# A two-layer decoder on one core: one table of steps per engine from the second half's expert tiles to the end of the third attention

## The reference

```python
x = x + _L0_attn_ref(_layernorm(x), ...)                      # gated recurrence and a gated FFN
x = x + _L0_xattn_ref(_layernorm(x), ctx_1024, ctx_1024, ...) # attention 1, over the context
x = x + _L0_ffn_ref(_layernorm(x), ...)                       # shared expert plus top 2 of 8 experts
x = x + _L1_attn_ref(_layernorm(x), ...)                      # attention 2, only the 24 strongest queries of a head
x = x + _L1_xattn_ref(ctx_1024, ctx_1024, _layernorm(x), ...) # attention 3, over the context
x = x + _L1_ffn_ref(_layernorm(x), ...)                       # top-1 experts with a capacity
```

```python
q_norm = jnp.sum(jnp.abs(q), axis=-1)
_, index = jax.lax.top_k(q_norm, u)            # u = 24
sel_attn = jax.nn.softmax(sel_scores, axis=-1)
attn_output = attn_output.at[bI, hI, index].set(jnp.einsum('bhut,bhtd->bhud', sel_attn, v))
```

## Time and profile before

| | us |
|---|---|
| median of three timed runs | 722.93 |
| lowest, highest | 719.76, 728.80 |
| the profiled execution | 720.38 |
| its span, first to last instruction | 718.7 |
| tiles of the second half | 299.4 to 342 |
| projections of the second attention | 342 to 394 |
| picks | 394 to 497 |
| third attention | 497 to 596 |
| what follows | 596 to 718.7 |

### The profile page before, as it was taken

The page is one execution under the profiler, slowest core; times in us unless marked ns, Lnnn a source line. Parts: engine busy times, 40 slices in busy tenths (PEclk is TensorE's granted clock), DMA queues, the critical chain, the costliest instruction groups (busy, mean ns, idle before and its releaser), DMA issues.

```text
span 718.7 us, 14894 instructions
## 1 busy us (share of the span) xinstructions
PE 569.8 (79%) x4679; PEld 413.6 (58%) x4679; DVE 434.5 (60%) x1157; ACT 290.9 (40%) x679; POOL 243.0 (34%) x364
## 2 busy tenths in 40 slices
PE   3689996889987979898727898876989984574992
PEld 1344444566764659897515686643666652454991
DVE  4879887666766575456373465554556624677443
ACT  2675422245555215454203466530435542302660
POOL 6745503301011666253640113224000002372652
PEclk9899999999999979999868899995999988577997
DMA  9974988653500166532301000363445300013114
GB/s 282 326 126 132 277 237 230 162 132 82 135 8 5 42 244 215 170 86 67 79 26 36 0 2 1 100 155 83 126 99 122 70 2 2 0 46 102 34 35 136
DMA packets 87494, 75.72 MB, mean 105 GB/s; under 512 B 10457, under 2 KB 80753, under 8 KB 84513
## 3 DMA queue, kind: packets, MB, share of 16 engines
q1 hardware_dynamic: 82544, 66.80, 34.5%
q0 software_dynamic: 3296, 6.79, 3.2%
q10 hardware_dynamic: 1584, 1.26, 0.6%
HBM read 41.59 MB, written 32.98 MB: 104 GB/s over the span
## 4 chain that ended last, share of the span: by engine, by line
PE 48%; DVE 20%; DMA 9%; issue 8%; POOL 6%; ACT 4%; SPq 3%; DVEq 1%; POOLq 0%; ACTq 0%
PE ps L2330 5%; PE ps L1864 5%; PE ps L2197 3%; PE ps L2162 3%; PE ps L2432 3%; PE ps L2444 3%; PE ps L2342 2%; PE ps L2181 2%; POOL xs_scr L839 2%; PE ps L2158 2%; DMA f<-k_scr 2%; SPq L433 2%; PE ps L2015 2%; PE ps L1860 2%; PE ps L2176 2%
## 5 line engine op out<-in xcount | busy, mean ns | idle before, releaser
L1445 DVE TENSOR_REDUCE negm<-ps 128x4 f32<-128x512 f32 x128 | 84.3, 688 | 57.1 <-PE ps L2162 53.9
L1026 ACT ACTIVATE wa<-ps 128x1024 f32<-128x1024 f32 x64 | 65.5, 1024 | 70.6 <-PE ps L2181 64.5
L2330 PE MATMUL ps<-nT,f 128*128 128x128 f32 x368 | 52.0, 288 | 2.6 <-DVE wb L1657 1.2
L2330 PEld LDWEIGHTS ps<-nT,f 128*128 128x128 f32 x368 | 47.9, 204 | 3.6 <-DVE wb L1657 1.6
L2197 PE MATMUL ps<-wa,f 128*32 128x128 f32 x1024 | 40.2, 284 | 4.0 <-ACT wa L1026 1.5
L1936 PE MATMUL ps<-identb 128*128 128x512 bf16 x100 | 34.2, 401 | 7.8 <-DVE negm L1445 3.9
L710 POOL DMA_INDIRECT x_scr<-y_tok,selT x32 | 31.9, 996 | 23.8 <-ACT stack L1134 10.7
L844 POOL DMA_INDIRECT y_scr<-f,stack x23 | 25.6, 1114 | 30.3 <-DVE f L1803 24.8
L2162 PE MATMUL ps<-stack 75*128 75x128 bf16 x352 | 35.6, 225 | 0.0
L2162 PEld LDWEIGHTS ps<-stack 75*128 75x128 bf16 x352 | 28.4, 101 | 12.2 <-issue 2.4
L1529 DVE COPY f<-w_gu 128x512 f32 x46 | 20.4, 442 | 22.0 <-issue 10.5
(11 more groups left out here) (399 smaller groups left out, 1464.8 us busy)
## 6 DMA issues: line engine op xcount, KB each, us to landing
k_scr<-parts SPq DMA_DIRECT2D x48, 192.0 KB, 3.0
q_scr<-parts SPq DMA_DIRECT2D x48, 192.0 KB, 2.8
stack<-k_scr SPq DMA_DIRECT2D x11, 600.0 KB, 7.2
stack<-q_scr SPq DMA_DIRECT2D x11, 600.0 KB, 5.5
w_w<-in_w SPq DMA_DIRECT2D x2, 2048.0 KB
wb<-q_scr SPq DMA_DIRECT2D x5, 600.0 KB
f<-k_scr SPq DMA_DIRECT2D x5, 600.0 KB
x_scr<-sel SPq DMA_DIRECT2D x2, 1472.0 KB, 10.2
```

Of the source, the lines that this page charges most:

```text
L1026: link.release(act.activation(wa[:, u % 2, :], BF[u % 2], ACT.Exp, scale=SCALE), hWA.filled, hWA.at(stage, n * 4 + u), hB.freed)
L1445: v.tensor_reduce(negm[:, g4 * 4:g4 * 4 + 4, j], A[u % 2].rearrange("p (h k) -> p h k", h=4), AX.X, ALU.max, negate=True).then_inc(hA.free ...
L2330: last = mm(A[x % 2][:, c * S:(c + 1) * S], gu_of[x % NGU][:, c * S:(c + 1) * S], nT[:, k % 2, q * S:(q + 1) * S], start=True, stop=True)
```

## The change

The loops from tile 23 to the end of the third attention are replaced by a third table, LATE, with one list for each of PE, ACT, DVE and POOL. All steps of the tiles (tg, td, tk on PE; ts, to, tn; tc, tp), of the projections (normx, turnx, evx, projq, projk, projv, tokq, heads, pick, turns, seld), of the picks (qp, pt, sc, tu, sv, pl; ex, ec, pu, at; pk, oq, lo, rc, ob; pf), of the output side and the next queries (outp, evo, back, res, stat2, rstd2, norm2, turn2, ev2, projq2, evq2, split2), of the gathers and their sums (ga, comb, stat, mrstd) and of the attention (A, B, M, V, X, o and their partners) stand in one order per engine.

So the first half's gathers are issued as soon as its rows are stored, its sums, statistics and normalisation stand among the second half's tiles, its projections follow the last tile, the picks of the first half run while the second half is gathered and projected, and the third attention's first scores run among the last picks. Normalisation moves from DVE to ACT (normx, with the mean's product in `from_mean`, two more small operations on POOL). The matmuls of `keep_warm` in the projections are gone. Memory is laid out anew: k1 and q1 lie in the stack, the picks' buffers over the gate and up weights, which adds waits for the last tile. In PSUM the first half's projections turn in three banks; the second half's, and the output side of blocks 0 to 2, take turns in bank Z, each waiting for the reader of the one before. `late_loads` has a new order and new waits.

```diff
-        k1 = [flat_gu[:, i * 2 * BT:(i + 1) * 2 * BT] for i in range(2)]
-        q1 = [flat_gu[:, (2 + i) * 2 * BT:(3 + i) * 2 * BT] for i in range(2)]
+        k1, q1 = ([room[:, (2 * i + k) * 2 * BT:(2 * i + k + 1) * 2 * BT] for i in range(2)] for k in range(2))
         spent = w["down"][:, :, :, :].rearrange("p e c d -> p (e c d)")
-        new_q, rest_q = [spent[:, s * BT:(s + 1) * BT] for s in range(2)], spent[:, 2 * BT:3 * BT]
-        pick32, q_bd, e_row, e_col, o_bd, put = ([room[:, (2 * k + s) * HU:(2 * k + s + 1) * HU] for s in range(2)]
+        pick32, q_bd, e_row, e_col, o_bd, put = ([flat_gu[:, (2 * k + s) * HU:(2 * k + s + 1) * HU] for s in range(2)]
                                                  for k in range(6))
-        pick16 = [room[:, 12 * HU + s * HU // 2:12 * HU + (s + 1) * HU // 2].bitcast(bf16) for s in range(4)]
+        pick16 = [spent[:, s * HU // 2:(s + 1) * HU // 2].bitcast(bf16) for s in range(4)]
...
+        def place(step):
+            kind, n = step[:-2], int(step[-1])
+            if kind in ("heads", "turns"):
+                return n
+            return (1 if n < 3 else 2) if kind in ("outp", "back", "turn2", "projq2") else n // 2
+        ORDER = {eng: FRONT[eng] + [s for s in WOVEN[eng] if not of_attention(s) and s[:2] not in ("fa", "fb")]
+                 + [s for s in LATE[eng] if s[:-2] in SIGNALS[eng]]
                  for eng in FRONT}
         PLACE = {step: (eng, i) for eng, steps in ORDER.items() for i, step in enumerate(steps)}
@@ -362,7 +366,23 @@
             assert len({PLACE[s][0] for s in steps}) == 1
             return max(PLACE[s][1] for s in steps) + 1
-        T_TURN = {s: k for k, s in enumerate(s for s in WOVEN["PE"] if s[0] in "MXo" and of_attention(s))}
+        T_TURN = {a: {s: k for k, s in enumerate(s for s in steps if s[0] in "MXo" and of_attention(s))}
+                  for a, steps in ((0, WOVEN["PE"]), (2, LATE["PE"]))}
+        three = (U, Bk[0][:, 0, :], Bk[1][:, 0, :])
+        first_turns, later_turns = ([s for s in LATE["PE"] if s[:-2] in READ_LATE and place(s) == n] for n in range(2))
+        def late_bank(step):
+            return (lambda: three[first_turns.index(step) % 3], lambda: Z, lambda: T)[place(step)]()
...
-                sp.wait_ge(qk1_ready, 1)
+                sp.wait_ge(gu_done, N0)
+                sp.wait_ge(pe_front, after("heads.1"))
                 load_k(a, 0, slot(0))
-                sp.wait_ge(qk1_ready, 3)
-                load_k(a, 2, slot(2))
                 store_pair("qp2", 0, queries, [], range(1))
                 sp.wait_ge(hP[0].freed, hP[0].free("qp2", 1))
+                sp.wait_ge(down_done, N0)
                 load_q(a, 0, slot(0))
+                sp.wait_ge(dve_front, after("comb.3"))
+                sp.wait_ge(slots_stored[1], 16 * PER)
+                load_k(a, 1, slot(1))
+                load_k(a, 2, slot(2))
                 store_pair("qp2", 0, queries, [], range(1, 2))
                 sp.wait_ge(hP[1].freed, hP[1].free("qp2", 1))
-                sp.wait_ge(attnT_done, 2 * B)
+                sp.wait_ge(scored, HB)
+                sp.wait_ge(q_picked, HB)
                 load_q(a, 1, slot(1))
-                load_k(a, 1, slot(1))
+                store_m(a, 0, slot(0))
+                sp.wait_ge(scored, B)
+                sp.wait_ge(q_picked, B)
                 load_q(a, 2, slot(2))
-                store_m(a, 0, slot(0))
+                store_m(a, 1, slot(1))
                 store_pair("qp2", 1, queries, [], range(1))
-                store_m(a, 1, slot(1))
+                load_stack(a, 3, slot(3))
+                store_m(a, 2, slot(2))
                 store_pair("qp2", 1, queries, [], range(1, 2))
-                for n in range(3, NSTEP):
+                for n in range(4, NSTEP):
...
+            def gathers(b):
+                h = b // HB
+                g.wait_ge(slots_stored[h], 16 * PER)
+                for k, dst in enumerate((y_tok, second)):
+                    g.indirect_dma_start(dst[:, b, :], None, x0_scr[h],
+                                         bass.IndirectOffsetOnAxis(ap=pos0_i[:, k * B + b:k * B + b + 1], axis=0))\
+                     .then_inc(rows_back[b // GB], 16)
+            def pick_copy(b):
+                g.wait_ge(gu_ready, N0)
+                g.wait_ge(pick16_ready, b + 1)
+                if b > 1:
+                    g.wait_ge(q_picked, b - 1)
+                g.tensor_copy(pick32[b % 2], pick16[b % 4]).then_inc(pick32_ready, 1)
...
-                    for n in range(NSTEP):
-                        for j in range(2):
-                            copies(n, j)
-                        if n == 0:
-                            late_step("h2", 3)
-                            late_step("s2", 2)
-                            late_step("s2", 3)
+                    for s in LATE["POOL"]:
+                        kind, n = s.split(".")
+                        if of_attention(s):
+                            copies(int(n), int(s[1]))
+                        elif kind == "clear":
+                            g.wait_ge(gu_done, N0)
+                            chain.settle()
+                            clear()
+                        elif kind == "ga":
+                            gathers(int(n))
+                        elif kind == "pf":
+                            pick_copy(int(n))
+                        else:
+                            late_step(kind, int(n))
...
-            for h in range(2):
-                if h == 1:
-                    for n in range(2):
-                        block_stats("qp1", n)
-                g.wait_ge(slots_stored[h], 16 * PER)
-                for b in range(h * HB, (h + 1) * HB):
-                    for k, dst in enumerate((y_tok, second)):
-                        if h == 0:
-                            g.wait_ge(slot_out, NT0 + b * TOPK + k + 1)
-                        g.indirect_dma_start(dst[:, b, :], None, x0_scr[h],
-                                             bass.IndirectOffsetOnAxis(ap=pos0_i[:, k * B + b:k * B + b + 1], axis=0))\
-                         .then_inc(rows_back[b // GB], 16)
-            for n in range(2, NBLK):
-                block_stats("qp1", n)
-            for b in range(B):
-                g.wait_ge(pick16_ready, b + 1)
-                if b > 1:
-                    g.wait_ge(q_picked, b - 1)
-                g.tensor_copy(pick32[b % 2], pick16[b % 4]).then_inc(pick32_ready, 1)
-                if b == 9:
-                    late_step("h2", 0)
-                elif b == 13:
-                    late_step("s2", 0)
-                    late_step("h2", 1)
-            late_step("s2", 1)
-            late_step("h2", 2)
...
+                if kind == "comb":
+                    v.wait_ge(rows_back[n], 16 * GB * TOPK)
+                    for k, src in enumerate((y_tok, second)):
+                        for b in range(n * GB, (n + 1) * GB):
+                            last = v.scalar_tensor_tensor(out=x_tok[:, b, :], in0=src[:, b, :], scalar=wts[:, k, b:b + 1],
+                                                          in1=x_tok[:, b, :], op0=ALU.mult, op1=ALU.add)
+                        link(last, settle=True)
+                    v.sem_inc(dve_front, 1)
...
+                this = "%s.%d" % (kind, n)
+                bank, where = late_bank(this), place(this)
+                if where == 2:
+                    settled("T")
+                    pe.wait_ge(q_bd_ready, B)
+                    pe.wait_ge(hT.freed, hT.at("ac2", T_next[0]))
+                    held["T"] = reader(this)
+                else:
+                    turns, depth = (first_turns, 3) if where == 0 else (later_turns, 1)
+                    turn_no = turns.index(this)
+                    if turn_no >= depth:
+                        read = reader(turns[turn_no - depth])
+                        pe.wait_ge(dict(ACT=act_front, DVE=dve_front)[PLACE[read][0]], after(read))
+                    elif where == 0:
+                        pe.wait_ge(dve_front, after("cc.1", "hd.3"))
+                        pe.wait_ge(act_front, after("sl.3"))
+                    else:
+                        pe.wait_ge(slot_out, N0 - 1)
...
-                keep_warm(T, 14)
-                pe.wait_ge(sel_ready, i + 1)
...
+LATE = {
+    "PE": """
+            td.21 td.22 tg.23 tk.7 tg.24 td.23 tg.25 td.24 tg.26 td.25 tg.27 tk.8 td.26 tg.28 tg.29 td.27 td.28
+            tg.30 tg.31 tk.9 tg.32 tg.33 td.29 tg.34 td.30 tg.35 tk.10 td.31 td.32 tg.36 td.33 tg.37 td.34 tg.38
+            td.35 td.36 tg.39 tk.11 tg.40 tg.41 td.37 turnx.0 td.38 td.39 td.40 tg.42 tg.43 td.41 td.42 tg.44 td.43
+            tg.45 td.44 turnx.1 projq.0 td.45 projk.0 projq.1 projv.0 tokq.0 heads.0 projk.1 projv.1 tokq.1 turns.0
+            pt.0 qp.0 pt.1 sc.0 qp.1 sc.1 tu.0 sv.0 tu.1 pl.0 sv.1 qp.2 pl.1 pt.2 sc.2 qp.3 pt.3 turnx.2 projq.2
```

(26 more changed lines are left out.)

## The result

The changed kernel took 686.3 us (median of four runs, 680.4 to 691.4) where the kernel before, beside it, took 722.0; the ratio is 0.946, 95% interval 0.935 to 0.958. The profiled execution took 682.5 us for a span of 680.7: 38.0 us less than the span before, where the prediction had 50.

A forecast was written before the change was run, and what follows sets the result against it. It saw room ahead of 497 us, where serial stages could overlap; gains of 36 us at the first pick, 18 at pick 8, 42 at the second step and 50 at the end gave 718.7 - 50 + 1.7 = 670.4, called 671 (range 652 to 697).

The forecast's parts named there:

- Part 6: Third attention: 91 us, to 546, against 99 before; gain at the end, where a 4 us hole closes.
- Part 1: First half's gathers without their per-tile waits: last gather 1.8 us earlier, nothing waits for it, costed at nothing.
- Part 2: Second half's tiles with the first half's statistics woven in: end at 346, bounds 337 and 349.
- The lock: Rival: VectorE copies lock GpSimd out of writing gather descriptors; +5 us, 676; chance 0.03.
- Part 3: First half's projections behind the tiles: first pick's query at 358, 36 us earlier than before.
- Part 4: Picks 0 to 7 with the second half's projections: pick 8 at 407 against 424.5, half of 36 us given back.
- the hole of 6 us: Before pick 2: TensorE loses 6 us because pick 2's copy stands behind GpSimd's gathers until 371.
- The 4 us lost at combination 3: Among picks: combination 3 waits for the last gather's landing (373.5), takes 3.1, and delays pick 2's maxima.
- Part 5: Picks 8 to 15 with third-attention queries: 41 us of work at 0.88 busy, 47; second step's scores at 455.
- The rival of one bank: Picks 8 to 15: turns through PSUM bank Z keep the old pace; +25 us, 696; chance 0.18.
- the clock's: Rival for Parts 3 to 5: TensorE stays at 1.2 GHz without keep-warm matmuls; +74 us, 745; chance 0.07.
- The rival of the loads: Third attention, steps 5 to 7: four stalls of 2.5 us waiting for loads; +10 us, 681; chance 0.08.

The follow-up runs named there:

- e11: Kernel before with only the per-tile waits of the first half's gathers taken out; ratio 1.001 to the kernel before.
- e1: Changed kernel with the first half's gathers again waiting for the second half's tiles; ratio 0.956 to the kernel before.
- e4: Changed kernel with the first half's sums, statistics and normalisation put behind the second half's last tile instead of among the tiles; ratio 0.965 to the kernel before.
- e10: Changed kernel with combinations 2 and 3 adding two rows instead of eight and statistics 2 and 3 not taken; profiled span 685.9 us.
- e5: Changed kernel with the third attention's old step order from step 2 on, the fourth block's queries still woven in; ratio 0.943 to the kernel before.
- e3: Changed kernel with unread matmuls added, 14 ahead of the first search's transposed selection and 36 ahead of pick 2's query; ratio 0.951 to the kernel before.

## Why the prediction was right, and where it was not

Faster by over 2% was right, the time lies in the range of 652 to 697, and the four marks from the tiles' end to step 2 came within 1.2 us of the forecast. Of the 12 us by which the span misses, 2.8 are the code ahead, 1.1 the code behind, 0.5 stand at step 2, and 7.6 are Part 6.

**Part 1** was right for the part alone (e11) and wrong for the change: the waits' end was priced at nothing in the order before, while Part 2 took the free gathers for granted (eight gathers landed by 321.9). e1 is the price of their sum, 11 us. The lock did not show: with tile copies beside them, fourteen of the sixteen gathers took 0.95 to 0.99 us and two 1.09 and 1.18, at 1.28 from one to the next. The Trainium skill (SBUF — State Buffer, "SBUF: two separate sides") would have descriptor writing locked out by such copies; the trace does not agree, beyond those 0.1 to 0.2 us on two gathers.

**Part 2** came to the right sum (48.6 against 48.4) by two errors that cancel, so by luck: the 23 tiles alone take 45.6 and not 39.4, and the woven steps cost 3.0 and not 9. (The 11.8 us of woven steps "with the wait" add up to 11.2 by its own terms: 4.5 from 320.5 to 325.0, then 1.8, 3.1 and 1.8.)

**Part 3** was right: 61.1 against 60.4, and e4 shows that 13 of those 36 us need the weaving; the other 23 remain without it.

**Part 4** gave the right time by a wrong cause. The copy of pick 2 came when it was forecast (374.65, 74.2 behind the transposes against 73.4), but the hole of 6 us with GpSimd in gathers does not exist: the same stretch is filled by two picks, priced at 7.1 us, which take 15.3 at 1.2 GHz. The mark of a clock above 0.9 from 376 on was right, but the 15 us ahead of it stood in no term. The 4 us lost at combination 3 are not there either. On VectorE's timeline it starts with no wait for the gathers' landing in front of it:

```profile
378.39 1.34 DVE L1362 SCALAR_TENSOR_TENSOR x_tok<-y_tok,wts,x_tok 128x128 f32<-128x128 f32 x4
```

TensorE had projections to do meanwhile, and leaving most of the sums out brings query 8 1.0 us earlier (e10).

**Part 5** was right in time, 47.5 us against 48, again by two sizes that cancel: 45.6 us of TensorE's work and not 41, at 0.96 busy and not 0.88, so no reader of Z held it up for long. The rival of one bank is out. So is the clock's: 1.00 from 376.8 to 536. Before, TensorE was busy 54.0 of the 72.9 us from query 8 on, at a clock of 0.90; no run tells how much of the 25 us gained is the clock's and how much the filled waits'.

```profile
424.54:497.40 72.86, 53.96 (x368) 40.35 (x366) 39.56 (x109) 32.58 (x118) 20.37 (x32) 0.90 0.32 83
```

**Part 6** failed, in its size: 89.9 forecast, 97.5 measured, as much as before. The terms that failed are those of the stage's end. Seven pitches took 77.0 us from the first score matmul of step 2 to the last of step 8, as forecast (77.7), though the fourth block's queries, priced at 2.6 apart from them, lie inside. Then 20.5 us follow up to the last row, in place of the 9.7 forecast (7.4 for the last step and 3 for the end, less the 0.7 behind that row). Windows of TensorE from the last score matmul to the last row (busy PE, PEclk, DMA, GB/s), of before, e11, e5 and the changed kernel:

```profile
576.20:595.40 19.20, 14.80 (x173) 0.82 0.01 2
585.30:601.20 15.90, 12.10 (x173) 1.00 0.01 3
544.40:560.20 15.80, 12.08 (x173) 1.00 0.01 2
535.80:556.40 20.60, 17.60 (x263) 0.95 0.01 2
```

The table runs the scores one and a half steps ahead of the sums, so that behind the last score group eight groups with maxima and ten sums stand, where the old order (before, e11, e5) has six and six: 5.5 us more of TensorE's busy time. And the hole that the table was to close belongs to one execution. In before's, TensorE waited 1.25 us for the last stored maxima and then ran at 1.2 GHz for 5.7 us; in e11, which leaves the attention as it is in before, the same instruction starts without a wait, at full speed:

```profile
582.82 0.61 PE L2176 MATMUL ps<-identb,fullmask 128*128 128x512 bf16 x1 [1.25 <-DMA stack<-mT]
```
```profile
590.63 0.39 PE L2174 MATMUL ps<-identb,fullmask 128*128 128x512 bf16 x1
```

So of before's 97.5 us some 3 were that execution's, and the old order can take 94.4. One line would have warned: TensorE is busy 88.8 us of the changed stage (90 before), and a forecast of 91 asks for 98% of it, where the stretch up to 536 has 92% and the tail 83%. The rival of the loads was right in kind and small: 1.2 us of one wait, and 0.3 of another.

## What to carry to other kernels

Price a wait in the order it will stand in, together with the other edits: what costs nothing before a rearrangement can be a ring of waits after it. Before forecasting a stage's new length, divide the bounding engine's busy time by it: at the same clock, no order of steps gives back more than the idle time that is there. Read the baseline of a stage from more than one execution: a hole in a single profile may be that execution's. And a mark hit to the microsecond proves no cause; moving the supposed cause does, and here three of them moved without moving the mark.

## What was not expected of the hardware

Unaltered code ahead of the change took 297.6 to 307.9 us, and the code behind it 123.3 to 129.0, from one execution to another. TensorE at 1.2 GHz looked busy (0.84 from 361.5 to 376.8, since each record is longer), and a mean clock of 0.89 in place of 0.50 shortened that stretch by 2.4 of 15.3 us (e3) and brought query 8 no earlier in any run beyond the spread. With one wait of 1.25 us and a stretch at 1.2 GHz behind it (582.8 to 588.5, clock 0.50), the end of the old attention took 3.3 us longer than in an execution that had neither.
